# Two gather layers of a graph network without the throwaway products behind the sums of slots

## The reference

```python
x = x + attention_dot(h, src, dst)            # layer 0: softmax over a node's edges
# layer 1: a gated unit on two means over neighbours
input_in  = mean over edges of (h @ W_in.T  + b_in)[src]   by dst
input_out = mean over edges of (h @ W_out.T + b_out)[dst]  by src
gi = concat(input_in, input_out) @ W_ih.T + b_ih
gh = h @ W_hh.T + b_hh
x = x + gated_unit(gi, gh, h)
# layer 2: a relation per edge
hW = einsum('nd,rde->rne', h, weight)                       # 8 relations
x = x + h @ sl_w.T + sl_b + segment_sum(hW[edge_type, src], dst) / deg
x = x + batch_norm(attention_additive(h, src, dst))  # layer 3
```

## Time and profile before

| what | value |
|---|---|
| timed runs | 9200.57, 9226.65, 9234.74 us; median 9226.65 |
| span of the profiled execution | 9189.2 us, 96642 instructions |
| TensorE, matmuls | 6435.8 us busy (70%), 25717 instructions |
| VectorE | 5548.1 us (60%) |
| ScalarE | 1640.5 us (18%) |
| GpSimd | 4507.2 us (49%) |
| DMA | 1012.59 MB, 110 GB/s over the span |

### The profile page before, as it was taken

The page is one execution under the profiler, slowest core; times in us unless marked ns, Lnnn a source line. Parts: engine busy times, 40 slices in busy tenths (PEclk is TensorE's granted clock), DMA queues, the critical chain, the costliest instruction groups (busy, mean ns, idle before and its releaser), DMA issues. The chain is left out here.

```text
span 9189.2 us, 96642 instructions
## 1 busy us (share of the span) xinstructions
PE 6435.8 (70%) x25717; PEld 3694.7 (40%) x25717; DVE 5548.1 (60%) x13040; ACT 1640.5 (18%) x5142; POOL 4507.2 (49%) x4616
## 2 busy tenths in 40 slices
PE   1477777777737666677777799866666677777774
PEld 1245555555423333344444444433333344444442
DVE  8778878888765655533333344433333666666667
ACT  0122222222210000000000055300000333333331
POOL 1024444444446766666666511366666244444440
PEclk9987777777768888888889899877777888888887
DMA  0354554445543333343333544433333533333334
GB/s 7 102 182 137 140 139 139 136 137 139 125 141 90 90 89 90 87 108 115 113 114 114 119 158 163 138 92 91 92 91 90 130 89 88 85 87 89 88 86 98
DMA packets 446254, 1012.59 MB, mean 110 GB/s; under 512 B 98365, under 2 KB 213609, under 8 KB 439076
## 3 DMA queue, kind: packets, MB, share of 16 engines
q0 software_dynamic: 240960, 702.53, 28.7%
q1 hardware_dynamic: 204772, 303.99, 10.1%
HBM read 845.67 MB, written 160.28 MB: 109 GB/s over the span
## 5 line engine op out<-in xcount | busy, mean ns | idle before, releaser
L718 PE MATMUL psum<-rows,oh 128*128 128x257 f32 (+2 forms) x8800 | 3084.5, 453 | 1276.9 <-issue 729.8
L718 PEld LDWEIGHTS psum<-rows,oh 128*128 128x128 f32 x8800 | 1671.6, 216 | 2571.7 <-issue 2340.1
L725 DVE TENSOR_TENSOR acc<-acc,psum 128x264 f32 (+2 forms) x3520 | 1485.0, 422 | 1518.3 <-PE psum L718 692.1
L814 PE MATMUL psum<-ident,ones 128*128 128x512 bf16 x4169 | 1662.2, 467 | 0.0
L697 POOL DMA_INDIRECT rows<-qv_tab,src_i x880 | 881.5, 1002 | 1574.0 <-PE psum L718 833.4
L697 POOL DMA_INDIRECT rows<-xh_tab,src_i x880 | 834.4, 948 | 994.3 <-PE psum L718 613.0
L697 POOL DMA_INDIRECT rows<-h_tab,src_i x880 | 890.9, 1012 | 436.8 <-issue 236.8
L697 POOL DMA_INDIRECT rows<-h_tab,wts x880 | 866.2, 984 | 442.4 <-issue 235.9
L697 POOL DMA_INDIRECT rows<-hw_tab,rel_i x880 | 870.6, 989 | 418.1 <-issue 237.6
L725 DVE TENSOR_TENSOR kh<-kh,psum 128x257 f32 x880 | 371.4, 422 | 793.3 <-PE psum L718 472.0
L874 PE MATMUL psum<-kh,oht 128*128 x1760 | 681.5, 527 | 1.3 <-ACT oht L987 1.3
(11 more groups left out here) (338 smaller groups left out, 7520.8 us busy)
## 6 DMA issues: line engine op xcount, KB each, us to landing
wts<-hots SPq DMA_DIRECT2D x220, 256.0 KB
hw_tab<-acc SPq DMA_DIRECT2D x50, 1024.0 KB, 4.1
part_tab<-rows SPq DMA_DIRECT2D x50, 512.0 KB
rows<-part_tab SPq DMA_DIRECT2D x50, 512.0 KB, 5.5
hots<-oh SPq DMA_DIRECT2D x74, 256.0 KB, 2.8
rows<-qv_tab,src_i POOLq DMA_INDIRECT x880
rows<-h_tab,src_i POOLq DMA_INDIRECT x880
rows<-h_tab,wts POOLq DMA_INDIRECT x880
```

Source lines behind the costliest of these rows:

```text
L718: nc.tensor.matmul(psum[:, banks[b % len(banks)], 0:width], oh[:, b // GROUP, b % GROUP], rows[:, b, at:at + width], start=True, stop=True ...
L725: nc.vector.tensor_tensor(to, to, psum[:, banks[b % len(banks)], 0:width], ALU.add).then_inc(acc_done, 1)
L814: nc.tensor.matmul(bank, ones[:, :].bitcast(BF16)[:, 0:P], busy, start=True, stop=True)
```

## The change

Both calls of `keep_warm` in the gather layers go. `gates_of` is called for the same slots and phases as before, and its answer isn't used any more. The attention layers keep theirs. Nothing else differs: the gathers, the sums, the waits and the order of the rest are the same.

```diff
@@ l1_tensor @@
             pe.wait_ge(ring[b], landed(j))
             aggregate(pe, j, b, 0, KHW)
-            if n < SLOTS or (n - SLOTS) // EACH >= TILES or not gates_of(*divmod(n - SLOTS, EACH)):
-                keep_warm(psum[:, 5, :], 1)
+            if n >= SLOTS and (n - SLOTS) // EACH < TILES:
+                gates_of(*divmod(n - SLOTS, EACH))
             what, at = due.get(n - 1) or (None, None)
@@ l2_tensor @@
             pe.wait_ge(ring[b], landed(j))
             aggregate(pe, j, b, 0, D)
-            keep_warm(psum[:, 0, :], 1)
```

## The result

The changed kernel takes 9205.75 us (median of 19 runs), the kernel before 9218.92 us in 19 runs beside it: a ratio of **0.9982, with an interval of 0.9975 to 0.9989**. Measured twice more, on different chips, the same pair gave 0.9966 (0.9954 to 0.9978) and 0.9970 (0.9957 to 0.9983). So the change gains 0.2 to 0.3%, 17 to 31 us by these ratios (the two medians stand 13 us apart), where 40 us more were forecast. The time lies in the range and within the 0.5% that were called no change, but its sign is the other one.

The account below looks back on a forecast made before the run. It took the TensorE-VectorE loop over two PSUM banks, with late `agg_done` signals, to hold GpSimd. Second layer +26, by-target half +10, by-source half +4 gave +40 us on a 9227 median, written as 9265; range 9040 to 9380.

Parts of the forecast that it names:

- The reading of the loop: Gather layers: GpSimd is held by the loop TensorE, VectorE, TensorE over two PSUM banks; 448 us is waiting for `agg_done`.
- A slow slot behind a hold: Second layer, TensorE at the low clock: without its throwaway product a slot goes from 1.28 to 0.96 us.
- Rival A: Fewer TensorE instructions a slot make its late `agg_done` signals rarer; a third of 448 us waiting goes, 9078 us; chance 0.33.
- Rival C: TensorE becomes the limit in the by-source half at a granted clock under 0.63; +143 us, 9370; chance 0.25.
- B: The forecast itself: clock falls in part, slow slots shorten, `agg_done` signals stay as late; 9215 to 9330 us; chance 0.42.
- the clock's price, +1.7 us a round: Second layer, round of 24 gathers: half of 13 fast slots lose the full clock, each going from 0.70 to 0.96 us.
- the forecast's zero for a late slot: Second layer, last part of a round, 7 slots of 2.79 us each: a late slot gains nothing from the removed product.
- The gain term: Second layer: three slow slots a round each gain 0.32 us without the product, -1.0 us a round, 37 rounds.
- The first layer: First gather layer: +10 us in the by-target half and +4 in the by-source half, from the same mix of clocks.
- the rule's result, +208 us: All gather stretches: by the skill's clock rule alone, the upper end everywhere, +208 us instead of +40.

Follow-up runs that it names:

- e5_keep: The changed kernel with the 430 throwaway products of the by-source half kept: 9222.36 us against 9236.13 for the kernel before, ratio 0.9977.

## Why the prediction was wrong

**The reading of the loop held.** 1979 products are left. A slow slot behind a hold takes 0.95 us without its product (forecast 0.96) and 1.07 and 1.71 with a small one and with two, a fast one 0.70 with or without. Rival A is refuted, since late additions are not rarer (second layer: 189 and 186 with the products, 206, 203 and 195 without). Rival C needed a by-source half with TensorE over 90% busy at a clock under 0.63; it is busy for 972 of 1319 us there, at 0.85, and `e5_keep` gained nothing by keeping its products. The late signals stayed about as they were, as B said.

**The step that failed is the clock's price, +1.7 us a round.** I counted all additions of the second layer by their distance from the one before and by the clock of their product (its records last 380 ns at the full clock, 634 at the low one). Means of two traces with and three without the products:

| distance | with: full clock | with: low | without: full clock | without: low |
|---|---|---|---|---|
| under 1.1 us | 355 in 249 us | 52 in 38 | 325 in 226 | 145 in 117 |
| 1.1 to 1.4 | 35 in 46 | 86 in 110 | 31 in 42 | 57 in 73 |
| 1.4 to 2 | 114 in 170 | 51 in 75 | 74 in 111 | 46 in 67 |
| 2 and more | 128 in 371 | 60 in 214 | 89 in 255 | 112 in 365 |

The forecast let half of 13 fast slots in each of 37 rounds lose the full clock, 240 in all, for 63 us. In fact there are only **355 - 325 = 30 fewer** of them, 0.8 a round, and 30 x 0.26 = 8 us. This is a net count, since slots change class: the fast slots at the low clock became 145 - 52 = 93 more, some of them slow slots that got shorter. Had all 93 lost the full clock, it would be 24 us. So I put the price at 8 to 24 us in place of 63, and with that the gain outweighs it and the sign turns. The loop behind a hold is dense enough for the full clock with its own two matmuls. I had seen that this part is the dense one and still took the middle between two ends, for want of a row. The row's hint was the better value.

**Where the clock went instead**: of the 188 late additions of before 60 had a low-clock product, of the 201 of after 112. Low-clock late slots are the longer ones, 3.57 us against 2.90 before and 3.26 against 2.87 after. But the mean of all late slots is 585/188 = 3.11 us before and 620/201 = 3.08 after, with almost twice as many at the low clock. So the lower clock did not lengthen them to be seen, and the forecast's zero for a late slot held; that the low-clock ones are longer may as well mean that a long wait is where the clock falls. The late part grew by 35 us with 13 more slots in it.

**The gain term** was about right in price and a little high in number: 111 slots of 1.28 were taken, and the table has 86 at the low clock between 1.1 and 1.4 us. With 86 x 0.32 = 28 us gained and 8 to 24 lost on fast slots the balance is -20 to -4 us, around the -14 measured. This agreement is not a proof: the class of 1.4 to 2 us fell by 67 us while the class under 1.1 grew by 56 and the late one by 35, so slots moved between the classes by more than these terms hold. That part is counted, not explained.

**The first layer** was put at +14, by the same clock term carried over, and measured +1. In the by-target half many slots are at the low clock now (0.66) and nothing gets longer. My reading, which no run tests, is that a slot there takes 1.50 us for GpSimd's and VectorE's sake, and the low clock's 0.95 fits in.

**The skill's rule.** The Trainium skill, page "TensorE: Matmul & The Clock Gate", Part 1, says that the throttled clock is the default and activity releases it. The traces agree (0.55 behind a hold, 1.00 in the dense part, 0.64 in the late one). What the forecast called the rule's result, +208 us, supposed that without the products there is no activity. The slots' own products were enough.

**How long the holds are** hardly answers to the loop's pace: a layer at 1274 us stays at 1269 with four banks. My reading was that a late phase lasts until GpSimd has been held, so that a faster catch-up leaves more room for lateness to fill. For it speaks that the first layer gains as soon as GpSimd waits at each gather; against it, that the second doesn't. It is not shown. **What makes the signals late stays open.** One cause that was not tried is the recording of the trace itself. The Trainium skill, page "NOTIFIC — the notification-queue block", section 7.1, says that the path that takes the engines' records pushes back when an internal FIFO fills, and that this can stall an engine; no run here shows it. The traces of the faster chip were recorded too and have no late signals, so the recording alone doesn't make them.

## What to carry to other kernels

Before pricing a lower clock, ask in which part of the loop it will be low. Here TensorE was dense by itself where it caught up and kept most of its clock there, and where it waited the lower clock cost nothing that the mean late slot shows. A throwaway product is worth its time only if a slot has that time to spare at the low clock; here one product is 0.33 us of a 1.28 us slot. Long slots with a slow clock don't show that the clock made them long: compare the mean over all of them before and after. And a loop that is made faster gains little if what holds it comes from elsewhere: changing one cost at a time (four banks, few bytes, other operand) tells this sooner than a sum does.

## What was not expected of the hardware

- The same kernel takes 8216 us on one chip and 9219 to 9236 on others. On the faster one GpSimd is never held in the gather layers, in the traces of four variants of the changed kernel; on the others it is held for 424 to 448 us, by the code always until `agg_done`.
- An indirect gather costs GpSimd 0.955 us for 64 rows and 0.994 for 128, and as much for rows of 64 bytes (880.25/880 = 1.00).
- A throwaway product of 64 columns still costs a low-clock slot 0.12 us.
- With four banks TensorE's records run ahead of its late signals, and the signals come no faster: additions in late slots begin 7.8 us behind the recorded end of their product in place of 3.8, and stay 3.5 us apart.
- At the low clock a slot's two matmuls take TensorE 0.85 us; with two banks the slot takes 0.95, with four the additions catch up at 0.63 on products already made.
